# A convolution block and a spline activation on one core: two opening sums moved from VectorE to ScalarE and an accumulating transfer, and two masks written earlier in each chunk

## The reference

```python
out = relu(batchnorm(conv3x3(x, sign(w1)), gamma1, beta1))
out = batchnorm(conv3x3(out, sign(w2)), gamma2, beta2)
s = relu(out + x)                                   # the sum that this change is about
x_aff = clip(s * a[c] + b[c], -1.5, 1.5)
u = (x_aff + 1) * 0.5 * 31
i, t = floor(u), u - floor(u)
spline = sum of alpha_table[i-1 .. i+2] * cubic_basis(t)       # 32 knots, 8 numbers each
y = id_gain[c] * s + einsum(spline, mix[c]) + bias[c]
```

## Time and profile before

| | us |
|---|---|
| median of three runs | 1139.02 (1136.41 to 1142.9) |
| the profiled execution | 1139.08 |
| its span in the profile | 1137.2 |
| TensorE busy | 1081.0 |
| VectorE busy | 966.2 |
| ScalarE busy | 899.3 |
| GpSimd busy | 137.5 |

### The profile page before, as it was taken

The page is one execution under the profiler, slowest core; times in us unless marked ns, Lnnn a source line. Parts: engine busy times, 40 slices in busy tenths (PEclk is TensorE's granted clock), DMA queues, the critical chain, the costliest instruction groups (busy, mean ns, idle before and its releaser), DMA issues.

```text
span 1137.2 us, 53175 instructions
## 1 busy us (share of the span) xinstructions
PE 1081.0 (95%) x24650; PEld 724.2 (64%) x24650; DVE 966.2 (85%) x959; ACT 899.3 (79%) x410; POOL 137.5 (12%) x195
## 2 busy tenths in 40 slices
PE   6999999699999968999999999999999999999996
PEld 5777777577777745556656656656666556656564
DVE  5856656687767779999999999999999998999997
ACT  4445443767777648999999999999999999999971
POOL 6000000058100000101101011011110110101100
PEclk9999999899999989999999999999999999999999
DMA  8677674677677936799898989989989988998652
GB/s 288 221 293 285 251 278 175 224 248 298 263 284 291 349 164 161 185 233 225 228 234 213 237 203 234 222 220 235 228 209 235 226 225 212 233 233 200 165 131 87
DMA packets 57465, 259.46 MB, mean 228 GB/s; under 512 B 16080, under 2 KB 16080, under 8 KB 49232
## 3 DMA queue, kind: packets, MB, share of 16 engines
q1 hardware_dynamic: 48496, 208.40, 54.6%
q0 software_dynamic: 8640, 48.17, 23.2%
q10 hardware_dynamic: 160, 0.30, 0.1%
HBM read 104.29 MB, written 77.07 MB: 159 GB/s over the span
## 4 chain that ended last, share of the span: by engine, by line
PE 86%; DVE 7%; issue 3%; DMA 1%; ACT 1%; SPq 0%; DVEq 0%; ACTq 0%
PE tab L1303 49%; PE acc L741 30%; PE tab L1313 7%; DVE middle_mask L1161 1%; DMA halo<-y_scratch 1%; DVE far_sq L1210 1%; DMA w_raw<-in_w 1%; ACT xin L381 1%; ACT yout L420 1%; DVE poly L1202 0%; DVE far L1188 0%; DVE stats L547 0%; DVE offset L1154 0%; DVE poly L1216 0%; DVE band_split L509 0%
## 5 line engine op out<-in xcount | busy, mean ns | idle before, releaser
L1303 PE MATMUL tab<-edge_mask,diag 128*32 128x392 bf16 x10240 | 446.6, 329 | 5.8 <-issue 2.5
L1303 PEld LDWEIGHTS tab<-edge_mask,diag 128*32 128x32 f16 x10240 | 283.5, 97 | 160.6 <-issue 20.1
L1058 ACT ACTIVATE edge_mask<-cell,thr 128x6272 bf16<-128x6272 bf16 x62 | 338.6, 5509 | 2.0 <-DMA cell<-cell 2.0
L420 ACT ACTIVATE yout<-acc 128x1568 f32<-128x1568 f32 x64 | 94.5, 1477 | 167.5 <-PE acc L741 146.9
L741 PE MATMUL acc<-band_split,w 64*64 64x385 f16 (+2 forms) x4608 | 194.6, 329 | 9.9 <-DVE band_split L509 4.9
L741 PE MATMUL acc<-split,w 64*64 64x385 f16 (+3 forms) x4608 | 191.5, 326 | 11.2 <-DVE w L468 10.0
L1303 PE MATMUL tab<-middle_mask,diag 128*32 128x392 bf16 x4096 | 187.2, 329 | 7.5 <-issue 5.5
L547 DVE BATCH_NORM_STATS2 stats<-yout 128x392 f32 (+1 forms) x240 | 117.9, 555 | 89.1 <-ACT yout L420 89.1
L741 PEld LDWEIGHTS acc<-band_split,w 64*64 64x64 f16 x4608 | 150.0, 109 | 54.3 <-issue 8.8
L741 PEld LDWEIGHTS acc<-split,w 64*64 64x64 f16 x4608 | 144.7, 108 | 57.1 <-issue 11.9
L1303 PEld LDWEIGHTS tab<-middle_mask,diag 128*32 128x32 f16 x4096 | 110.6, 97 | 72.6 <-DVE middle_mask L1161 10.4
(11 more groups left out here) (140 smaller groups left out, 962.0 us busy)
## 6 DMA issues: line engine op xcount, KB each, us to landing
y_scratch<-yout SPq DMA_DIRECT2D x32, 1568.0 KB, 6.2
cell<-cell SPq DMA_DIRECT2D x496, 98.0 KB, 4.6
xin<-y_scratch SPq DMA_DIRECT2D x16, 1568.0 KB, 6.2
lin<-far POOLq DMA_DIRECT2D x32, 784.0 KB, 8.6
out<-lin SPq DMA_DIRECT2D x31, 784.0 KB, 5.3
xin<-in_x SPq DMA_DIRECT2D x15, 1568.0 KB, 6.5
lin<-y_scratch SPq DMA_DIRECT2D x30, 784.0 KB, 9.3
lin<-in_x POOLq DMA_DIRECT2D x28, 784.0 KB, 7.9
```

What stands on the lines that cost most here:

```text
L420: act.activation(yout[b][:, :].rearrange("p (r k x) -> p k r x", r=2, k=TILES)[:, 2 * part:2 * part + 2], acc[:, 4 * part:4 * part + 4, 0: ...
L1058: act.activation(mask_of(c, q)[:, :, :], cell4[c % 2][:, :, :], ACT.Sign, bias=thr[:, q:q + 1]).then_inc(sign_mask_ready, 1)
L1303: mm = pe.matmul(tab[(c + t) % 2][j * GROUP:(j + 1) * GROUP, sub, 0:SUB], keep["diag"][part][:, j % 2, t, q, :], mask_of(c, q)[:, j, sub * ...
```

## The change

1. `AHEAD` falls from 4 to 2, and a new constant `EARLY_CHUNKS` = 4 keeps the early loads of `y2` for four chunks. The early loads of `x` for chunks 2 and 3 are gone. The sums of these two chunks are now made as those of later chunks: `scale(2)` and `scale(3)` on ScalarE, `add_x(2)` and `add_x(3)` on GpSimd's queue, and `position(2)` and `position(3)` wait for the additions. `total(2)` and `total(3)` are gone from VectorE. `x_added` becomes two semaphores.
2. The loads of `y2` for chunks 4 and 5 no longer wait for the four sums, since `lin4` and `lin5` held no `x`.
3. The middle masks wait for a new semaphore `middle_used`, which TensorE raises after the last matmul of FAR on a middle mask, and not for the whole FAR table.
4. In VectorE's order of the chunks from 1 on, the first middle mask moves from behind `far_part` to the place ahead of `far_cube`, and the second from behind `slope` to the place behind `far_part`. In chunk 0 the order of the masks stays.

```diff
-AHEAD = 4
+AHEAD = 2
+EARLY_CHUNKS = 4
@@ last round of the convolution stage, SP
-                    for c in range(AHEAD):
+                    for c in range(EARLY_CHUNKS):
...
                         sp.dma_start(y_to[:, :], y2[c // 2][:, px]).then_inc(keep["y_loaded"][c], 16)
-                        sp.dma_start(x_to[:, :], x[c // 2][:, px]).then_inc(keep["x_loaded"][c], 16)
+                        if c < AHEAD:
+                            sp.dma_start(x_to[:, :], x[c // 2][:, px]).then_inc(keep["x_loaded"][c], 16)
@@ spline, SP, load(c)
-                if c < LIN:
-                    sp.wait_ge(sum_ready, AHEAD)
@@ spline, GpSimd
-                pool.dma_start(lin_of(c)[:, :], image_half(x, c), accum_op=ALU.add).then_inc(x_added, 16)
+                pool.dma_start(lin_of(c)[:, :], image_half(x, c), accum_op=ALU.add).then_inc(x_added[c % 2], 16)
...
+            add_x(2)
             for c in range(CHUNKS):
-                if AHEAD <= c + 3 < CHUNKS:
+                if c + 3 < CHUNKS:
                     add_x(c + 3)
                 add_far(c)
@@ spline, ScalarE
             cells(1)
+            scale(2)
             distance(0)
             far_distance(0)
             far_square(0)
+            scale(3)
             position(2)
@@ spline, VectorE
-                dve.wait_ge(table_ready, used(c - 1, T_FAR))
+                dve.wait_ge(middle_used, c)
...
-            total(2)
             near_cube(0)
             fixed(2)
-            total(3)
             far_cube(0)
...
                 near_cube(c)
                 finish(c - 1)
+                if c + 1 < CHUNKS:
+                    middle(c + 1, MIDDLE_QUADS[0])
                 far_cube(c)
                 far_part(c)
                 if c + 1 < CHUNKS:
-                    middle(c + 1, MIDDLE_QUADS[0])
+                    middle(c + 1, MIDDLE_QUADS[1])
                 square(c)
                 if c + 1 < CHUNKS:
                     offsets(c + 1)
                 slope(c)
-                if c + 1 < CHUNKS:
-                    middle(c + 1, MIDDLE_QUADS[1])
                 add_slope(c)
@@ spline, TensorE, table(c, t)
+                    if t == T_FAR and q == MIDDLE_QUADS[-1]:
+                        mm.then_inc(middle_used, 1)
```

9 lines of the change are left out of this document (5 added, 4 removed).

## The result

The changed kernel takes 1142.51 us (median of 22 runs, 1136.28 to 1148.95) against 1138.94 for the kernel before (22 runs on the same chip, 1135.28 to 1142.9). The ratio is 1.0040, 95% interval 1.0027 to 1.0053: 0.4% slower, inside the range and inside the band of 0.5% that was called no change. The profiled execution took 1143.17 us, its span is 1141.4; before it was 1137.2.

A forecast was written before the change was run, and what follows sets the result against it. The prediction took TensorE (86% of the chain that ended last) to bound the kernel. It summed 1139.08 + 2.3 + 1.35 - 3.0 = 1139.7 us, no change, with a range of 1135.5 to 1143.5.

The forecast's parts named there:

- The lock-out of GpSimd: Opening: GpSimd gets no turn between VectorE's first masks, so its issue for chunk 2 ends with them at 434.2.
- The rival with a turn between two masks: Opening: GpSimd gets in near 432.1, far_cube(0) costs 0.6 us instead of 2.3, total 1138.0; chance 0.25.
- The landing: Opening: chunk 2's addition lands 6.4 us after its issue ends, at 440.6, and position(2) can then start.
- `far_cube(0)` later by 2.3: Chunk 0: far_cube(0) starts at 443.3 instead of 441.04, and all 2.3 us reach VAL and the masks of chunk 1.
- The edits at nothing: Opening: scale(3), later edge(1), add_x(3) and earlier loads cost nothing; if their covers failed, 1 to 2 us more.
- Masks in chunk 1, 1.35: Chunk 1: both masks ahead of square(1) start it 1.76 us later; NEAR of chunk 2 loses 1.35 us.
- The rival on the clock: Chunk 0: TensorE's clock falls in the longer pause, costing up to 5 us, total 1144.7; chance 0.05.
- No mask awaited, chunks of 21.20: From chunk 2 on: no mask is awaited and steady chunks read 18.57 + 2.63 us.
- The rival of a replaced wait: Steady chunks: the wait moves to near_cube or far_cube, chunks stay at 21.31 us, total 1142.7; chance 0.12.
- The 3.0 gained in steady chunks: The 30 later chunks: 0.11 us gained in about 26, 0.1 in two more, 3.0 us together.
- First middle mask waits for copies, slower: Later chunks: the mask ahead of far_cube waits for cell-tile copies; 0.2 us late per chunk gives over 1145; chance 0.05.
- Other pauses change: TensorE's pauses without an awaited semaphore, about 9 us, change: fall of over 5 us chance 0.06, equal rise 0.05.

The follow-up runs named there:

- second comparison: The changed kernel, unchanged, timed and traced once more beside the kernel before: 1141.7 us, ratio 1.0033.
- the filled one: The changed kernel plus 64 small unused matmuls behind LIN of chunks 0 and 1, second run: 1142.44 us, ratio 1.0050 to the kernel before.
- sums only: Kernel before with only the sums of chunks 2 and 3 moved to transfers, masks in old order with old wait: 1141.7 us, ratio 1.0026.
- chunk 2's sum only: Kernel before with only chunk 2's sum moved to ScalarE and the transfer, masks as before: 1144.27 us, ratio 1.0050.
- chunk 3's transfer alone: Kernel before with only chunk 3's sum made by transfer and the masks early from chunk 2 on: 1141.21 us, ratio 1.0036.
- masks only: Kernel before with only the masks released and written earlier, all four sums on VectorE: 1139.74 us, ratio 1.0018.
- masks from chunk 2 on: Kernel before with the masks early only from chunk 2 on, all four sums on VectorE: 1140.91 us, ratio 1.0012.

## Why the prediction held, and where it did not

The time was in the range and the change below 0.5%, as forecast. But the forecast stood 0.6 us above the kernel before, and the two kernels were 3.6 apart (and 3.3 in the second comparison): a real if small loss, and one that the sum had at almost nothing. At 1142.51 the time is 1.0 below the upper end of the range, which was that wide for the spread of runs and for a rival that did not come true. That it held is in part luck. Step by step:

- **The lock-out of GpSimd.** "By this row the issue ends with the masks at 434.2" was wrong for the profiled execution: it ended at 432.40. The rival with a turn between two masks was right on the issue. But it is not settled by the program: the issue lasted 1.34 in four traces and 3.24 and 3.23 in two, each time beside two pairs of masks. The changed kernel (1.34) and the filled one (3.23) have the same program on both engines. The Trainium skill ("SBUF — State Buffer", section "Who interferes with whom") calls the shared ports an exclusive lock; all six issues ended 0.1 us behind a VectorE mask pair, which agrees, and in two of them the lock was not passed on at the boundary.
- **The landing.** "From the end of the issue that is 6.4" was the other error: it was 8.5 to 8.8 after the short issues (in the changed kernel 431.06 + 9.96 less 432.40), and 7.4 and 8.1 after the long ones. The two errors cancelled, which was luck. I had named the longest landing (11.2), but took that of a transfer at 460 us, beside which SP's queue moved 168 packets; the changed kernel's first transfer had 407 beside it, and in the trace of before the two with 365 and 405 landed in 10.1 and 10.4. The first addition took 9.96 us, just inside the 10 from which on I had called myself wrong; in sums only (11.3), chunk 2's sum only (10.2) and the filled kernel (10.6) it was outside.
- **`far_cube(0)` later by 2.3**: 2.74 measured, the term came out near the sum's for the wrong reason. It reached VAL of chunk 0 as I said (452.16, forecast 451.7). Of it 2.6 to 2.8 arrived at i1, in two traces. But the pause of 3.5 that I had put ahead of VAL came in two parts, 1.34 in FAR and 2.09 ahead of VAL (0.80 and 2.64 in the second trace). The first is again a thing that I had at nothing, hidden here in VectorE's lateness.
- **The edits at nothing.** `scale(3)` and `add_x(3)` do cost: the transfer holds up the copies of chunk 1 by some 4 us. In the whole change this is hidden behind `far_cube(0)`; alone it costs 2.3 to i1, partly by a fall of the clock.
- **Masks in chunk 1, 1.35, the step that failed.** `square(1)` started 4.51 later than before, of which 2.74 are from the sums and 1.77 from the second mask (forecast 1.76). The wait was 2.43, forecast 2.6. The mechanism was right and the term too small, since it left out what the clock does behind such a wait: the 64 products took 1.67 longer (4.51 less 2.84). Both together are the 3.0 that both traces show from i1 to i2. So the term of 1.35 was mis-sized, and 3.0 is what stands in its place. The rival on the clock was put in chunk 0 at a chance of 0.05; in six traces with a transfer for chunk 2 it fell there in three (sums only, chunk 2's sum only, filled), once also with chunk 3's transfer alone, and in chunk 1 in all three traces that had the new order there and no filling.
- **No mask awaited, chunks of 21.20**: right, from chunk 2 on. The rival of a replaced wait is out.
- **The 3.0 gained in steady chunks.** The undisturbed chunk is 21.21 in all eight traces with the new order and 21.31 or 21.32 in all five with the old one, so the gain is there. What of it reaches the end is less sure: from i3 to i31 the four traces with the new order from chunk 1 on have a mean of 605.1, the five with the old order 607.5, but the four with the new order from chunk 2 on have 608.3.
- **First middle mask waits for copies, slower**: nothing of it is in the traces.
- **Other pauses change.** Those without an awaited semaphore behind 500 us were 9.2 before and 10.3 after, so they did not move by 5. Yet one of 2.80 at 744.31 brought a fall of the clock, and in three other kernels one of 2.62 to 2.82 between 654 and 660 did.

The sum with the measured terms is 2.7 + 3.0 - 3.0 = 2.7 for the whole change; measured were 4.6 and 3.8 (ratios 1.0040 and 1.0033), with intervals of 3.1 to 6.0 and 1.4 to 6.0. A like shortfall, of 2 to 4 us, is in the kernels with early masks alone: masks only should come to 0 by this count and measured +2.0 (0.1 to 3.9), masks from chunk 2 on to -2.4 (0.6 - 3.0) and measured +1.4 (-0.3 to +3.0).

**What stays open** is this part. The rest column leans to longer pauses with the new order (a mean of 12.8 in eight traces, 10.8 in five with the old), but the spread of one kernel is 3, so this is not shown; and C, which ranges over 3.2 us from trace to trace, could hide a part as well.

What the pauses are, on the other hand, the kept traces do show. In the stretch 741 to 747 us of the changed kernel, around the pause of 2.80 that ended at 744.31, the DMA view has two packets of the instruction queue:

```profile
q8 instruction: 2, 0.03, 2.2%
```

The first was under way from 741.94 to 743.06, and TensorE went on 1.25 later. Taken alone this says little, since such a packet comes every 6 us or so. But behind 430 us the thirteen traces have 148 pauses of TensorE of over 0.15 us without an awaited semaphore, and every one of them ended 1.1 to 1.7 us after a packet of this queue had landed. Of its 65 pauses with an awaited engine only 6 ended 1.0 to 1.8 us after one, and of moments taken at random one in seven lies there. So these are waits for packets of the instruction queue, which by its name carries the program's own code.

The traces also show what went on before: in the 3 us before such a packet started, the queue of the accumulating transfers took 68% of the DMA engines' time (the median of 146 packets), before the other 1363 packets 2%. In the opening this can be told apart by kernel. All six traces with a transfer for chunk 2 have a pause of 0.80 to 1.89 us in FAR of chunk 0 (1.34 in the changed kernel, its packet under way from 438.46 to 439.57), and none of the seven without it has one there. That the transfer is what makes the packet late is an argument from these two counts; no kernel here changed the code or its place.

## What to carry to other kernels

An opening with idle DMA engines can still have a transfer on its path: before a sum is moved from an engine to an accumulating transfer, count the transfer from its issue to its landing beside the traffic of just that stretch, and ask which small copies it will delay. Freed time on an engine is worth nothing until the transfer's landing, so the first chunk whose data can wait is the one to start with. A wait of TensorE that grows to the lengths that had a fall here (2.20 to 3.50 us, though 2.45 and 2.64 had none) should be priced twice, once for itself and once for a possible fall of the clock behind it; and an order that is better in the steady state costs its difference once, in the chunk where it is taken up while the engine is behind.

## What the runs showed of the hardware

- The clock falls in or just behind short pauses. Pauses of 2.20, 2.43, 2.57 (twice), 2.62, 2.75, 2.80, 2.82, 2.99 and 3.50 us came with 3 to 7 us at 0.50 (two of 1.43 and 1.72, nine products apart, did as well); pauses of 2.02, 2.09, 2.15, 2.17, 2.45 and 2.64 did not. The length alone does not tell which.
- The same GpSimd issue, started 0.8 us into a pair of VectorE masks of 1.97 together, lasted either 1.34 or 3.24 us, by execution.
- The first accumulating transfer of 784 KB landed 9.9 to 11.3 us after its issue's start with some 400 or more packets of copies beside it, and 7.6 in the earlier trace rows with 168; the copies' own landing went from 2.2 to 5.6 us.
- TensorE's pauses without an awaited semaphore, 5.6 to 11.9 us in sum behind 500 us, all ended 1.1 to 1.7 us after a packet of the instruction queue (148 of 148), and in the 3 us before those packets the queue of the accumulating transfers took 68% of the DMA engines' time (median), before all others 2%.
